# A second stage with its scales computed in one piece, and the first half's rows moved after the second half's block sums

## The reference, cut to what matters

```python
x = x + conv(ln(x), protein_pair, compound_pair, z_mask, ...)   # x: 256 x 64 x 128
t = x.reshape(16384, 128)
x = t + ffn(ln(t), Wr, br, ln_g, ln_b, W1, b1, W2, b2)

def conv(z, ...):
    z = layernorm(z)
    ab = sigmoid(z @ gate_w + gate_b) * (z @ lin_w + lin_b) * z_mask     # 256 x 64 x 64
    g = sigmoid(z @ eg_w + eg_b)
    block1 = einsum('bikc,bkjc->bijc', protein_pair, ab)
    block2 = einsum('bikc,bjkc->bijc', ab, compound_pair)
    return g * (layernorm(block1 + block2) @ as_w + as_b) * z_mask

def ffn(x, ...):    # 8 experts, each token goes to its best two
    probs = softmax(x @ Wr + br)
    weights, idx = top 2 of probs, divided by their sum
    y_e = gelu((norm(x) * g_e + b_e) @ W1[e] + b1[e]) @ W2[e] + b2[e]
    return sum of weights * y_idx
```

## Time and profile before

| | |
|---|---|
| median of 3 runs | 990.55 us (989.59 to 992.62) |
| the profiled execution's own time | 992.77 us |
| its span, first to last instruction | 990.9 us |
| mean granted TensorE clock | 0.879 of 2.4 GHz |
| busy, share of the span | PE 76%, PEld 66%, DVE 64%, ACT 61%, POOL 59% |
| DMA | 124.21 MB, mean 125 GB/s |

### The profile page before, as it was taken

One profiled execution on the slowest core, in us unless ns is written; L12 is line 12 of the kernel. 1 busy time (PEld: TensorE's weight loads), 2 busy tenths in 40 slices (PEclk: granted clock), 3 DMA queues, 4 the chain that ended last, 5 costly groups with the idle time before them and its releaser, 6 DMA issues.

```text
span 990.9 us, 24898 instructions
## 1 busy us (share of the span) xinstructions
PE 752.3 (76%) x7186; PEld 657.3 (66%) x7187; DVE 634.3 (64%) x2187; ACT 603.4 (61%) x1247; POOL 583.5 (59%) x547
## 2 busy tenths in 40 slices
PE   2788895667594674358098989989939989899893
PEld 1677794556493463312088879888938988898793
DVE  5766404996704898562187878878826767667572
ACT  1868895564594554401086768777817867777681
POOL 4545101543177886887545766767754767767674
PEclk9989997798797687755588999999989999999897
DMA  9993305474013246441133443434324434434420
GB/s 255 329 326 113 92 1 170 146 218 146 5 57 128 90 138 202 135 150 68 55 96 106 133 125 106 127 111 137 103 65 128 128 108 137 128 99 128 120 86 19
DMA packets 124019, 124.21 MB, mean 125 GB/s; under 512 B 21886, under 2 KB 91415, under 8 KB 123963
## 3 DMA queue, kind: packets, MB, share of 16 engines
q1 hardware_dynamic: 90212, 80.24, 28.5%
q0 software_dynamic: 15296, 34.64, 10.1%
q10 hardware_dynamic: 18456, 8.67, 3.1%
HBM read 77.21 MB, written 48.68 MB: 127 GB/s over the span
## 4 chain that ended last, share of the span: by engine, by line
PE 57%; POOL 14%; DVE 12%; issue 10%; ACT 3%; DMA 2%; SPq 1%; DVEq 0%; ACTq 0%; POOLq 0%
POOL row_dram L475 7%; PE ps L1219 6%; PE ps L1220 6%; PE ps L1221 6%; PE ps L1239 6%; PE ps L1242 6%; PE ps L1240 6%; PE ps L1081 6%; POOL row_dram L464 4%; PE ps L1198 4%; PE ps L1132 3%; POOL rs L454 2%; PE ps L1233 2%; DVE stats L888 1%; DVE work L949 1%
## 5 line engine op out<-in xcount | busy, mean ns | idle before, releaser
L1038 DVE TENSOR_TENSOR rows<-ABz,rows 128x512 f16<-128x512 f32 x280 | 193.9, 693 | 93.6 <-ACT rows L691 91.4
L513 POOL DMA_INDIRECT row_dram<-PPb x140 | 160.2, 1144 | 89.3 <-DVE PPb L1047 49.0
L516 POOL DMA_INDIRECT out<-PPb x140 | 160.6, 1147 | 84.6 <-DVE PPb L1047 45.3
L690 ACT ACTIVATE ABz<-ps 128x512 f32<-128x512 f32 x280 | 169.0, 603 | 54.5 <-PE ps L1221 46.4
L1239 PE MATMUL ps<-PPb,rows 128*128 x1120 | 187.9, 222 | 0.0
L1240 PE MATMUL ps<-PPb,rows 128*128 x1120 | 187.7, 221 | 0.0
L691 ACT ACTIVATE rows<-ps 128x512 f16<-128x512 f32 x280 | 170.0, 607 | 0.0
L1219 PE MATMUL ps<-B,PPb 128*128 128x256 f16 x560 | 157.2, 281 | 4.2 <-issue 4.2
L1220 PE MATMUL ps<-B,PPb 128*128 128x256 f16 x560 | 157.2, 281 | 0.0
L1221 PE MATMUL ps<-B,PPb 128*128 128x256 f16 x560 | 157.1, 281 | 0.0
L1242 PE MATMUL ps<-PPb,rows 128*128 x1120 | 155.7, 221 | 0.0
(11 more groups left out here) (233 smaller groups left out, 1549.7 us busy)
## 6 DMA issues: line engine op xcount, KB each, us to landing
PPb<-row_dram SPq DMA_DIRECT2D x70, 264.0 KB, 2.8
PPb<-in_L_conv_protein_pair SPq DMA_DIRECT2D x32, 512.0 KB, 6.2
PPb<-row_dram SPq DMA_DIRECT2D x70, 136.0 KB, 2.6
rows<-in_x SPq DMA_DIRECT2D x32, 256.0 KB, 6.3
g_dram<-work ACTq DMA_DIRECT2D x32, 256.0 KB, 2.4
work<-g_dram SPq DMA_DIRECT2D x32, 256.0 KB, 2.8
ABT<-in_x SPq DMA_DIRECT2D x32, 256.0 KB, 3.0
row_dram<-PPb POOLq DMA_INDIRECT x140
```

The costliest lines, as they stand in the source:

```text
L513: pool.indirect_dma_start(row2_dram, bass.IndirectOffsetOnAxis(ap=Rw[:, u, b, POS:POS + 1].bitcast(u32), axis=0), Rw[:, u, b, :], None, bo ...
L516: pool.indirect_dma_start(out_rows, bass.IndirectOffsetOnAxis(ap=Rw[:, u, b, TOK:TOK + 1].bitcast(u32), axis=0), Rw[:, u, b, 0:D], None, b ...
L690: act.activation(Hf[:, u % 2, q, :], full, ACT.Gelu, scale=1.0 / SCALE)
L1038: dve.tensor_tensor(rest[:, part], Hf[:, u % 2, q, :], high[:, part], ALU.subtract).then_inc(h_parts[q], 1)
```

## The change

The second stage is rewritten, and GpSimd's part in it removed:

- **Scales of B at once.** VectorE takes all statistics of `B` and computes all scales and shifts in two pieces (`scale_b`: groups 0 to 3, then 4 to 15), with x^-0.5 by an integer estimate and three Newton steps on VectorE (`MAGIC`), into `bsc`. The second piece runs behind `gate_b(1)`. GpSimd's `power` is gone.
- **x1 goes straight into `rows`** (no copy by ScalarE); in the second half `gate_b(n)` waits for that group's move ahead of its second operation. Its statistics are taken at once; the variances are computed for a whole batch at the head of `choose` (16 new steps, `STATS`).
- The loops over groups are written out. `SPLIT` is 32; `choose(1)` runs behind `gate_b(11)`.
- `weights(0)` moves on ScalarE from ahead of the `ABT` copies to behind the tenth pair copy, `ranks(0)` on TensorE to behind the second group of products.
- GpSimd in the second half: waits for all block sums, masks and padding, then all 16 groups of moves, then the scatters.
- SyncE loads W1, W2 and the rest behind group 8 of the second half. TensorE folds four experts ahead of the table.

```diff
-SPLIT = 28
+SPLIT = 32
-AHEAD = 7
+MAGIC = float(0x5F3759DF)
...
@@ SyncE
-                    wait_reuse(sp, s.x1_kept, n, 4, GH * h)
-                    wait_reuse(sp, s.x1T_psum, n, 4, GH * h)
+                    wait_reuse(sp, s.x1_done, n, 4, GH * h)
...
+                for n in range(GH):
+                    load_gates(n, n % 4)
                     if h == 0:
                         pp_piece(1, n)
+                    if h == 1 and n == GH // 2:
+                        sp.dma_start(W1s, W1.rearrange("e d h -> d e h")).then_inc(fw_loaded, 16)
+                        sp.dma_start(W2s, W2.rearrange("e (k p) d -> p e k d", p=P)).then_inc(fw_loaded, 16)
...
@@ GpSimd
-                    pipeline(pool, GH, 2, [((0, X1LAG), power)])
-                    pool.wait_ge(s.tail, 12)
+                    pool.wait_ge(s.tail, 1)
                     set_keep(0)
                 else:
-                    for g in range(AHEAD):
-                        move_rows(g)
                     pool.wait_ge(s.blk_done, 2 * PAIRS)
                     set_keep(1)
                     set_keep(2)
...
-                    for i in range(STEPS):
-                        power(i, i % 2, [i < GH, i >= X1LAG])
-                        if i % 2 == 0 and AHEAD + i // 2 < GH:
-                            move_rows(AHEAD + i // 2)
-                        if i == GH:
-                            pool.wait_ge(s.tail_done, 2)
-                        if i >= GH:
-                            scatter(TG * (i - GH), TG * (i - GH + 1))
-                    scatter(TG * X1LAG, SPLIT)
+                    for g in range(GH):
+                        move_rows(g)
+                    pool.wait_ge(s.tail_done, 2)
+                    scatter(0, SPLIT)
                     pool.wait_ge(s.tail_done, 3)
                     scatter(SPLIT, NC)
...
@@ ScalarE
                         blk_copy(q // 4 - 1)
+                        if h and q == 10:
+                            weights(0)
...
-                    act.activation(rows[:, bass.ds(n * TG, TG), 0:D], gr[:, u, :, :], ACT.Copy).then_inc(s.x1_kept, 1)
...
+                for t in range(GH + 6):
+                    if t < GH:
+                        norm_b(t)
+                    if 0 <= t - 1 < GH:
+                        bT_copy(t - 1)
+                    if 0 <= t - 4 < GH:
+                        x1T_copy(t - 4)
+                    if 0 <= t - 6:
+                        logit_copy(t - 6)
+                    if h and t == SPLIT // TG + 6:
+                        weights(1)
...
@@ VectorE, choose
+                dve.wait_ge(s.x1_stat, GH * h + j1 // TG)
...
+                for _ in range(3):
+                    tail(dve.tensor_tensor(sq, y, y, ALU.mult))
+                    tail(dve.tensor_tensor(sq, sq, hv, ALU.mult))
+                    tail(dve.scalar_tensor_tensor(y, sq, 1.5, y, ALU.add, ALU.mult))
...
@@ VectorE, second stage
+                def scale_b(j0, j1, i):
...
+                    for _ in range(3):
+                        bstep(dve.tensor_tensor(sq, y, y, ALU.mult))
+                        bstep(dve.tensor_tensor(sq, sq, hv, ALU.mult))
+                        bstep(dve.scalar_tensor_tensor(y, sq, 1.5, y, ALU.add, ALU.mult))
+                    bstep(dve.tensor_tensor(bsc[:, 0, j0:j1], y, mask, ALU.mult))
+                    bstep(dve.tensor_tensor(m1, m1, bsc[:, 0, j0:j1], ALU.mult))
+                    dve.tensor_tensor(bsc[:, 1, j0:j1], m1, mask, ALU.add).then_inc(s.b_ready, 1)
...
+                def gate_b(n):
...
+                    dve.tensor_tensor(gr[:, n % 4, :, :], v, gr[:, n % 4, :, :], ALU.mult).then_inc(s.as_mul, 1)
+                    if h:
+                        dve.wait_ge(moved[n % 4], (n // 4) * (16 * TG) + 16 * TG)
                     dve.wait_ge(s.as_mul, n + (1 + g0))
+                    dve.tensor_tensor(rows[:, n * TG:(n + 1) * TG, 0:D], gr[:, n % 4, :, :], xk[:, n % 4, :, :], ALU.add).then_inc(s.x1_done, 1)
+                    dve.wait_ge(s.x1_done, n + (1 + g0))
+                    for t in range(TG):
+                        i = dve.bn_stats(x1st[:, n * TG + t, :], rows[:, n * TG + t, 0:D])
+                    i.then_inc(s.x1_stat, 1)
...
+                scale_b(0, HEAD * TG, stat_b(0, HEAD * TG))
+                stat_b(16, 32)
+                gate_b(0)
+                stat_b(32, 48)
+                gate_b(1)
+                scale_b(HEAD * TG, NC, stat_b(48, NC))
+                for n in range(2, GH):
+                    gate_b(n)
+                    if h and n == SPLIT // TG + 3:
+                        choose(1)
                 choose(2 * h)
@@ TensorE
-                if h:
-                    ranks(0)
                 pe.wait_ge(s.abT_copied, h * 8 + 8)
...
+                    if h and m == 1:
+                        ranks(0)
...
+            pe.wait_ge(s.am_done, 1)
+            for e in range(4):
+                fold(e)
             pe.wait_ge(s.Q_done, 1)
```

More of the change, by code:

```diff
@@ L236, in __init__ @@
                 self.base = take(base, NG)
+                self.stat = take(stat, 11 * nj)
         flat = PPb[:, :, :].rearrange("p a b -> p (a b)")
@@ L446, in _ @@
             for h in range(IC):
[L447 to L454, removed]
                 def move_rows(n):
@@ L593, in _, with weights @@
                     act.wait_ge(s.cp_done, 2)
+                def weights(b):
+                    _, j0, j1 = BATCHES[b]
+                    act.wait_ge(s.tail, TAIL * b + STATS + 15)
+                    for col, scale in ((WLO, 1.0), (WHI, -1.0)):
+                        a = act.activation(rows[:, j0:j1, col:col + 1].rearrange("p j o -> p (j o)"), choices[b].m12[:, DL, :],
+                                           ACT.Sigmoid, scale=scale)
+                    a.then_inc(s.w_given, 1)
                 act.wait_ge(pp_loaded[h], 16 * 16)
+                if h:
+                    act.wait_ge(s.tail, 1)
                 def blk_copy(m):
@@ L653, in _, with bT_copy @@
-                pipeline(act, GH, 4, [(0, await_norm), (1, bT_copy), (0, norm_b),
-                                      (6, await_logit), (4, x1T_copy), (6, logit_copy)],
-                         after=(GH - 1, lambda: weights(1)) if h else None)
+                def bT_copy(n):
+                    act.wait_ge(s.bT_psum, n + (1 + g0))
+                    wait_reuse(act, s.as_done, n, 2, g0)
+                    act.activation(bT[:, n % 2, :], ps[n % 2][:, 0:256], ACT.Copy).then_inc(s.bT_copied, 1)
@@ L669, in _ @@
                     a.then_inc(s.am_done, 1)
-                weights(2 * h)
+                    weights(2)
             for e in range(NE):
@@ L811, in choose @@
+                sh, dv = (rows[:, j0:j1, q:q + 1].rearrange("p j o -> p (j o)") for q in (SH, RS))
+                dve.tensor_scalar(dv, y[:, 1, :], 1.0, None, ALU.mult)
+                tail(dve.tensor_tensor(sc[:, 0, :], sc[:, 0, :], y[:, 1, :], ALU.mult))
+                assert tails[0] == TAIL * b + STATS
+                dve.tensor_scalar(sh, sc[:, 0, :], 1.0, None, ALU.add)
                 dve.wait_ge(s.logit_done, GH * h + j1 // TG)
-                dve.wait_ge(s.x1T_copied, GH * h + j1 // TG)
@@ L953, in _, with bstep, stat_b @@
-                pipeline(dve, GH, 4, [(X1LAG, gate_b), ((0, X1LAG), statistics), ((1, X1LAG + 1), deviations)],
-                         after=(GH, lambda: choose(1)) if h else None)
+                steps = [0]
+                def bstep(i):
+                    i.then_inc(s.b_step, 1)
+                    steps[0] += 1
+                    dve.wait_ge(s.b_step, steps[0] + h * 2 * 18)
+                def stat_b(j0, j1):
+                    for j in range(j0, j1):
+                        i = dve.bn_stats(bst[:, j, :], B[:, j, :])
+                    return i
@@ L1163, in logit @@
                     for t in range(TG):
-                        i = pe.matmul(ps[6][:, t * P:(t + 1) * P], x1T[:, u % 2, t, :], Wr_ident[:, 0:P], start=True, stop=True)
+                        i = pe.matmul(ps[6][:, t * P:(t + 1) * P], x1T[:, n % 2, t, :], Wr_ident[:, 0:P], start=True, stop=True)
                     i.then_inc(s.logit_psum, 1)
-                pipeline(pe, GH, 4, [(0, bT), (1, as_mm), (3, x1T_mm), (5, logit)],
-                         after=(GH - 1, lambda: ranks(1)) if h else None)
+                for t in range(GH + 5):
+                    if t < GH:
+                        b_trans(t)
+                    if 0 <= t - 1 < GH:
+                        as_mm(t - 1)
+                    if 0 <= t - 3 < GH:
+                        x1T_mm(t - 3)
+                    if 0 <= t - 5:
+                        logit(t - 5)
+                    if h and t == SPLIT // TG + 6:
+                        ranks(1)
                 if h:
@@ L1180, in _ @@
             i.then_inc(s.tbl_psum, 1)
-            pe.wait_ge(s.am_done, 1)
-            for e in range(NE):
-                if e >= 4:
-                    pe.wait_ge(s.f_step, 2 + e - 4)
```

(5 more changed lines are left out.)

228 lines of the change are left out of this document (88 added, 140 removed).

## The result

The changed kernel takes **952.91 us** (median of 4, 952.43 to 955.49), the kernel before on the same chip 991.59 (median of 4): ratio 0.9614, 95% interval 0.9583 to 0.9644. Forecast: 952. The profiled execution took 953.16 us, its span is 951.4.

A forecast was written before the change was run, and what follows sets the result against it. GpSimd's queue, and behind it the end of the second half's block sums, was taken to set where the experts start. From 990.55: -26.2 - 7.9 - 5.3, +1 for moves beside busy VectorE, gives 952 us; low 943, high 966.

The forecast's parts named there:

- a: First half's second stage: x1 of group 15 done at 224 us, against 238.65 before.
- rival 3: First half's second stage bound by VectorE alone: x1 at 218 instead of 224, 942 to 945 us; chance 0.15.
- Rival 2: TensorE stays at 1.2 GHz in the first half's second stage: +24 us, 976; chance 0.06.
- b: From x1 to the block sums: they start 26.8 us earlier and end at 276.6 instead of 302.8, -26.2 us.
- c: GpSimd from block end to first scatter: masks 2.1 us, 64 moves at 1.264 pitch, sum 85 us, 7.9 less.
- The tie: Before the first scatter: choice 1 reaches its indices near 358, last move lands near 361; 3 us late costs 3.
- d: GpSimd's scatters: 85.4 us instead of 90.7, as 5.3 us of powers and their gaps go.
- e: Experts' preparation: ends by 435, or 12 us before the last scatter.
- Rival 4: Something other than GpSimd's last scatter holds the experts: 30 us late gives 970 us; chance 0.04.
- Rival 1: VectorE's two-input steps block GpSimd's issues of moves and scatters: 46 us, 998, slower; chance 0.04.

The follow-up runs named there:

- e11: Changed kernel with weights and ranks of choice 0 put back ahead of the second half's ABT copies: 965.61 us, kernel before 992.07, ratio 0.9729.
- e9: Changed kernel again, no edit, in a second session: 952.22 us, kernel before 989.84, ratio 0.9623.
- e1: Changed kernel with weights and ranks of choice 0 put back ahead of the ABT copies, disturbed session: 1104.49 us, kernel before 1098.21, ratio 1.005.
- e2: Kernel before with only weights and ranks of choice 0 moved late, disturbed session: 1085.54 us, kernel before 1098.21, ratio 0.9877.
- e4: Kernel before with all its moves put behind the block sums, disturbed session: 1101.38 us, kernel before 1098.21, ratio 1.0028.
- e5: Changed kernel with five groups of moves ahead of the second half's masks, disturbed session: 1091.02 us, ratio to kernel before 0.9941.
- e8: Changed kernel with both passes of scales ahead of gate 0, disturbed session: 1089.08 us, ratio to kernel before 0.9921.
- e10: Changed kernel with five groups of moves ahead of the masks and expert weights loaded behind all gates, disturbed session: 1109.70 us, kernel before 1115.82, ratio 0.9948.
- e12: Changed kernel with five groups of moves ahead, expert weights behind all gates, SPLIT 28, both scale passes ahead of gate 0, disturbed: 1099.33 us, ratio to kernel before 0.9853.
- e3: Changed kernel with one unused power of 12 columns on GpSimd ahead of each group of moves, disturbed session: 1075.23 us, ratio to kernel before 0.9742.
- e7: Changed kernel with W1, W2, b1 and the rest loaded behind all gate loads, disturbed session: 1086.17 us, ratio to kernel before 0.991.

## Why the prediction was right, point by point

- *a, the second stage.* Forecast 224, measured 220.82 (220.13 + 0.69): between the forecast and rival 3's 218. VectorE's own pace was right (2.44 us a group until DMA holds it, 2.42 forecast); DMA's limit showed in the last four groups only. Rival 3 fails by those: without their waits x1 would be done near 218.4 (an estimate, all at 2.44). Rival 2 is out: the granted clock is 1.00 from 189.5 on, and the stage's window has 0.86.
- *b, from x1 to the block sums.* Forecast -26.2, measured **-32.2** (270.6 for 302.8): the largest mis-sized term. Three of the six us come from a. Last x1 to last logit is 5.4 us (226.23 - 220.82), not 6, and transposes and ABT copies are 5.4 (to 231.67), not 7.5. The 6.5 taken for the copies came from a stretch at the lower granted clock: TensorE, out of work from 250 on until the weights were computed, was granted 0.50 from 252.5 to 262.7, and the copies wait for its transposes. Now no such gap stands ahead of them and the clock is 1.00. The kernel before, then the changed one (columns as above):

```profile
250.00:255.00 5.00, 0.00 (x0) 0.00 (x0) 4.76 (x8) 0.00 (x0) 0.00 (x0) 0.75 0.00 0
255.00:260.00 5.00, 1.44 (x7) 1.47 (x8) 4.79 (x13) 1.69 (x5) 1.08 (x2) 0.50 0.00 0
```

```profile
225.00:230.00 5.00, 4.10 (x32) 3.31 (x33) 4.62 (x14) 3.09 (x7) 0.00 (x0) 1.00 0.00 0
```

The eight copies start 0.85 us apart before (257.83 to 263.81) and 0.67 now (226.46 to 231.18); in e11, where the wait is back, 0.92, at a granted clock of 0.50 from 240 to 246. From first pair copy to end 38.9 us, 39.1 forecast. e11 shows the mechanism itself.
- *c, GpSimd's moves.* Forecast 85, measured 87.7 (270.58 to 358.26). Masks 2.1 as forecast. The pitch over 63 intervals is 1.307, not 1.264: 2.7 us. The tie was well seen: choice 1 is through L864 at 355.56, the last move lands for 357.44, so the moves win by 1.88 us. The gates did follow the moves, with 16.1 us of waits in 7 gates, but not at the 5.06 us that I gave: one waited 6.06 us, and from 315.24 to 337.24 they came 4.40 us apart. It cost nothing, as the moves won. (By the forecast's own numbers the last landing is 1.0 us beyond its slot, 2.3 less 1.264, not the 1.3 written there; the 2 us of the sum measured 1.9.)
- *d, the scatters.* Forecast 85.4, measured 87.1 (358.26 to 445.40), again the stretched issues. Choice 2 was done at 386.5, the 33rd scatter started at 399.93: 13 us of slack, 11 forecast.
- *e, the preparation.* 430.45, forecast by 435. Rival 4 is out.
- *The sum.* -32.2 - 5.2 - 3.5 + 1.4 (experts) = -39.5, as the span has it (990.9 to 951.4). Forecast -38.4. So the hit of 1 us is in part luck: the start was forecast 6 us too late, the queue and the experts 5 us too cheap, and the errors cancel. The order's part, 15.0 us at the pair copies and some 12 at the end, is shown by e11; the share of each part of the second stage, of the powers and of the moves behind the block sums is read from the traces only.

**Rival 1, the port, is half right.** The trace shows what it had wrong. An issue beside a VectorE step with PSUM as one input takes 0.96 us. One that starts inside a step whose two inputs are both in SBUF is stretched, but not if the step has only just begun (284.35):

```profile
284.31 0.77 DVE L924 TENSOR_TENSOR rows<-work,ABT 128x512 f32<-128x512 f32 x1
284.35 0.96 POOL L449 DMA_INDIRECT row_dram<-rows,idx  x1 [0.30 <-issue]
...
287.92 0.68 DVE L920 TENSOR_TENSOR work<-ps,work 128x512 f32<-128x512 f32 x1
288.14 0.96 POOL L449 DMA_INDIRECT row_dram<-rows,idx  x1 [0.30 <-issue]
...
298.19 0.69 DVE L924 TENSOR_TENSOR rows<-work,ABT 128x512 f32<-128x512 f32 x1
298.27 1.44 POOL L449 DMA_INDIRECT row_dram<-rows,idx  x1 [0.31 <-issue]
...
302.23 0.69 DVE L924 TENSOR_TENSOR rows<-work,ABT 128x512 f32<-128x512 f32 x1
302.55 1.21 POOL L449 DMA_INDIRECT row_dram<-rows,idx  x1 [0.30 <-issue]
...
401.20 5.76 POOL L460 DMA_INDIRECT row_dram<-rows,idx  x1 [0.30 <-issue]
401.24 4.88 DVE L991 SCALAR_TENSOR_TENSOR PPb<-PPb 128x512 f16<-128x512 f32 x8
...
425.90 1.21 DVE L1001 TENSOR_TENSOR ABz<-ABz 1x1024 f32<-1x1024 f32 x1
426.30 1.67 POOL L460 DMA_INDIRECT row_dram<-rows,idx  x1 [0.30 <-issue]
```

At 298.27 the step has 0.61 us to go and the issue is 0.48 longer; at 302.55 0.37 and 0.25; at 426.30 0.81 and 0.71. An issue that is held thus waits for the rest of the step less some 0.12 us. At 284.35 the issue starts 0.04 us behind the step's start: it takes its 0.96, and the step takes 0.77 where the 15 others of L924 take 0.69. In the four undisturbed traces (before, after, e9, e11) 74 issues of moves and scatters start inside such a step with over 0.15 us of it to go. Of these 51 are held, and all start 0.047 us or more behind the step's start; of the 23 others 22 start 0.043 us behind it or less, and one, with 0.16 us to go, is 0.03 longer.

Two cases don't fit. The issue at 401.20 starts 0.04 us ahead of the first of L991's eight steps, which follow each other without a pause, and still waits for all eight: 4.92 us to go, 4.80 longer. One at 424.97 is 0.06 longer inside a step with one SBUF input (L997). These two and 18 held ones are the 20 issues of 1.00 us or more, the first move left out; together they are 2.4 us longer in the moves and 7.5 in the scatters (4.8 of them L991's; before it was 4.0). My rival charged every such step whole (46 us), my forecast nearly nothing; reading only the 5 us one as an exception was the error in both.

The Trainium skill ("SBUF — State Buffer", section "Who interferes with whom") has the rule that a VectorE instruction with two SBUF inputs contends with GpSimd's reads, and that issue order decides who blocks. The trace agrees where the issue comes second, at 10 us of this kernel. Where the issue comes first it doesn't: 11 of the 16 steps of L924 start 0.18 to 0.95 us into an issue and take 0.69 us like the rest.

## What to carry to other kernels

Where one engine's queue (here GpSimd's 128 issues) leads to the end without slack, find what its first element waits for: work that an engine has ahead of that only by program order, such as weights nobody needs yet, costs nearly its whole wait at the end, and moving it is a cheap gain (some 12 of 39 us here). Take copy and transpose times from a stretch at the granted clock that they will have, not from behind an idle gap. An indirect DMA's issue here paid for a two-input SBUF step only if it started inside one (or right ahead of an unbroken run of them), so count the odds of that, not the steps.

## What the runs showed of the hardware

**The disturbed sessions.** Up to GpSimd's first row moves their traces agree with the others to about 1 us (masks at 284.47 in e1, 285.27 in e11). Then, while GpSimd issues the moves without pause, the other engines issue their instructions slowly. The same kernel and windows, columns as above, e1 (disturbed):

```profile
300.00:320.00 20.00, 1.44 (x8) 0.99 (x7) 6.17 (x31) 0.00 (x0) 15.13 (x17) 0.59 0.32 106
320.00:340.00 20.00, 0.00 (x0) 0.00 (x0) 1.90 (x9) 0.00 (x0) 15.13 (x17) 0.50 0.16 54
```

and e11:

```profile
300.00:320.00 20.00, 8.44 (x42) 7.32 (x41) 17.14 (x79) 6.13 (x18) 15.20 (x16) 0.64 0.48 146
320.00:340.00 20.00, 15.54 (x100) 13.26 (x99) 9.48 (x28) 13.41 (x42) 15.42 (x16) 0.91 1.00 327
```

VectorE's timeline in e1 there, steps that depend on nothing but VectorE:

```profile
326.61 0.23 DVE L887 BATCH_NORM_STATS2 work<-B 128x6 f32<-128x64 f32 x1 [1.17 <-issue]
328.01 0.23 DVE L887 BATCH_NORM_STATS2 work<-B 128x6 f32<-128x64 f32 x1 [1.17 <-issue]
337.84 0.24 DVE L898 TENSOR_TENSOR work<-work 128x48 f32<-128x48 f32 x1 [9.60 <-remote]
...
365.13 0.21 DVE L913 TENSOR_TENSOR work<-work,bsc 128x48 f32<-128x48 f32 x1 [1.19 <-DVE bsc L912]
```

Dependent steps of 0.21 us come every 1.40 us, in e11 every 0.24; GpSimd's own pitch is 1.27. The last move starts at 366.5, and from 377 on a group takes VectorE 2.3 us again, as in e11. The same holds for the block sums: in e2 (moves beside them) TensorE is busy 17.00 of 33 us, in e4 (no moves there) 32.96:

```profile
270.00:303.00 33.00, 17.00 (x104) 14.77 (x104) 0.00 (x0) 11.75 (x13) 24.93 (x27) 0.69 0.16 56
```

```profile
270.00:303.00 33.00, 32.96 (x284) 31.85 (x283) 0.00 (x0) 32.24 (x35) 0.00 (x0) 1.00 0.00 1
```

Undisturbed, with the moves beside, it was 29.99 of 30. GpSimd waits for choices 1 and 2 together 65 to 82 us in e1, e5 to e8, e10 and e12, but 22 in e3, whose powers leave pauses between groups of moves: from 320 to 340 TensorE is busy 12.60 us there and in e7, in the same stage, 0.00; the experts, with indirect DMAs of their own, take 573 us in e7 instead of 503. DMA was not full (0.16 to 0.32 of its time in e1's two windows). What makes the issue slow is open. The delivery of instructions is one candidate, and the traces give it no support as far as they show it: of the instruction packets that they hold, those between 200 and 480 us take 0.3 to 1.4 us in e1 and e7 and 0.3 to 1.3 in e11, and e1 has none from 320 to 387, where the step of 1.40 us is. Whether a chip or the moment has it is open too, but the record gives the same chip number, 4, for e9 (undisturbed) and, five minutes later, for e10 (disturbed); if that is one and the same chip, it is the moment. For a kernel that must be fast there as well, e3 suggests pauses between indirect DMAs: its ratio, 0.974, is the best of the disturbed runs, though the changed kernel without the powers was not run beside it.
